# Mixer: a new order within a step for exponentials, products, taps and the shared kernels

## The reference

```
proj = rmsnorm(x) @ in_proj_w.T            # gate | hid, B, C | dt
hid, B, C = silu(causal_conv(hid_B_C))     # 4 taps along the tokens
L = exp(segsum(A * dt))                    # decay between tokens, per head
M = (C @ B.T) * L                          # per head; C @ B.T is shared by a group
y = M @ (hid * dt) + D * hid
yg = y * silu(gate); yg = yg * rsqrt(mean over a group of yg**2)
out = x + (yg * gnorm_w) @ out_proj_w.T
```

## Time and profile before

| | us |
|---|---|
| median of 3 runs | 2763.43 (2762.61 to 2765.62) |
| the profiled execution's own time | 2761.49 |
| its span in the trace | 2759.7 |
| TensorE busy | 2324.9 (84% of the span) |
| VectorE busy | 1963.2 (71%) |
| ScalarE busy | 1463.1 (53%) |
| GpSimd busy | 1210.6 (44%) |

### The profile page before, as it was taken

One profiled execution on the slowest core, in us unless ns is written; L12 is line 12 of the kernel. 1 busy time (PEld: TensorE's weight loads), 2 busy tenths in 40 slices (PEclk: granted clock), 3 DMA queues, 4 the chain that ended last, 5 costly groups with the idle time before them and its releaser, 6 DMA issues. The chain is left out here.

```text
span 2759.7 us, 33994 instructions
## 1 busy us (share of the span) xinstructions
PE 2324.9 (84%) x11172; PEld 1681.7 (61%) x11172; DVE 1963.2 (71%) x3158; ACT 1463.1 (53%) x3097; POOL 1210.6 (44%) x772
## 2 busy tenths in 40 slices
PE   5957767666523999999999999999999999889997
PEld 4532222225512767777767767777777777568996
DVE  4569989984434786686685685766765866778777
ACT  2344444433102795595685775866855956742221
POOL 2129988971000363363462553543634633541112
PEclk9989999988666999999999999999999999889999
DMA  2030030000041241231231321312312312220110
GB/s 80 22 123 0 0 122 0 0 28 34 27 152 64 90 124 54 73 118 49 86 95 54 96 83 61 110 55 79 111 55 72 115 54 73 73 78 24 47 47 31
DMA packets 117378, 183.59 MB, mean 67 GB/s; under 512 B 9760, under 2 KB 77728, under 8 KB 116192
## 3 DMA queue, kind: packets, MB, share of 16 engines
q1 hardware_dynamic: 117216, 181.55, 20.7%
HBM read 170.90 MB, written 10.62 MB: 66 GB/s over the span
## 5 line engine op out<-in xcount | busy, mean ns | idle before, releaser
L78 PE MATMUL mg_pb<-xT2h,mg_wh 128*128 128x512 f32 x1152 | 482.1, 419 | 17.0 <-POOL mg_wl L1265 17.0
L79 PE MATMUL mg_pb<-xT2l,mg_wh 128*128 128x512 f32 x1152 | 457.7, 397 | 0.0
L80 PE MATMUL mg_pb<-xT2h,mg_wl 128*128 128x512 f32 x1152 | 455.9, 396 | 0.0
L1275 POOL TENSOR_TENSOR mg_y<-mg_hT,mg_sg 128x512 f32<-128x512 f32 x128 | 175.6, 1372 | 633.7 <-DVE mg_hT L1510 633.7
L784 PE MATMUL ss_y<-ss_pr,cst 128*128 128x512 f32 x512 | 280.4, 683 | 123.5 <-POOL ss_pr L766 123.4
L1460 DVE SCALAR_TENSOR_TENSOR mg_hT<-mg_pb,mg_cw,mg_hT 128x510 f32<-128x510 f32 (+2 forms) x432 | 314.0, 739 | 30.3 <-ACT mg_hT L1615 24.6
L766 POOL TENSOR_TENSOR ss_pr<-o,ss_bc 128x1024 f32<-128x1024 f32 x128 | 301.3, 2369 | 46.2 <-DVE o L735 23.7
L1487 DVE TENSOR_TENSOR mg_m<-mg_gb,mg_cb 128x384 f32<-128x384 f32 x512 | 265.0, 549 | 74.8 <-ACT mg_gb L1665 72.2
L784 PEld LDWEIGHTS ss_y<-ss_pr,cst 128*128 128x128 f32 x512 | 100.0, 212 | 303.9 <-POOL ss_pr L766 222.0
L666 ACT ACTIVATE ss_da<-dt,ss_na 128x510 f32 (+1 forms) x256 | 165.9, 680 | 207.9 <-DVE o L735 207.9
L78 PEld LDWEIGHTS mg_pb<-xT2h,mg_wh 128*128 128x128 f32 x1152 | 220.1, 191 | 78.7 <-issue 18.8
(11 more groups left out here) (291 smaller groups left out, 5214.9 us busy)
## 6 DMA issues: line engine op xcount, KB each, us to landing
mg_abc<-acs_rows SPq DMA_DIRECT2D x256, 256.0 KB, 3.3
mg_ws<-in_w_in SPq DMA_DIRECT2D x72, 512.0 KB, 3.7
ss_bc<-bc_rows SPq DMA_DIRECT2D x16, 1024.0 KB, 6.3
mg_wos<-in_w_out SPq DMA_DIRECT2D x64, 256.0 KB, 4.0
ff_ws<-in_w SPq DMA_DIRECT2D x7, 1024.0 KB, 4.8
x<-in_x SPq DMA_DIRECT2D x16, 256.0 KB, 4.4
ip_ws<-in_w_in SPq DMA_DIRECT2D x8, 512.0 KB, 3.6
x_kept<-x SPq DMA_DIRECT2D x2, 2048.0 KB, 7.2
```

Of the source, the lines that this page charges most:

```text
L78: pe.matmul(out, lhs[0], rhs[0], start=start, stop=False)
L79: pe.matmul(out, lhs[0], rhs[1], start=False, stop=False)
L80: return pe.matmul(out, lhs[1], rhs[0], start=False, stop=stop)
L1275: pool.tensor_tensor(yb[:, p % RING, t], hT[s % 2][:, t], sg[s % 2][:, t], ALU.mult).then_inc(s_y2, 1)
```

## The change

The same operations are computed; only their places in the hand-written orders change, and one wait is added.

- VectorE, steps that finish a pair: `clamp(p, 1)` goes to the head of the step; products 2 and 3 come straight behind 0 and 1, ahead of the second `times_step` and of all taps; products 6 and 7 come ahead of the output tile's add and both skips; the second weight's low part goes behind the first skip. The taps of a half tile stay together.
- ScalarE there: decay 2 and 3 ahead of `high` and of the first tap; decay 6 and 7 ahead of the second `high`.
- B/C: the taps of C's second half (j = 3) and the four silus of B and C move into the next step, r = 1.
- r = 1 on TensorE: the first output tile ahead of `square_sums`, and `shared_kernels` behind the third projection. On VectorE `shared_out` goes behind the second `low`; on ScalarE `root` behind the second `high`.
- `clamp` waits for the group's table (`s_step`) where it is the first to need it.

```diff
--- before.py
+++ after.py
@@ -1429,13 +1429,12 @@
                     proj(s, 1, 0)
                     proj(s, 1, 1)
                     if outs:
+                        out_tile(*outs[0])
                         square_sums(s // PS - 1)
+                    proj(s, 2, 0)
+                    proj(s, 2, 1)
                     if not is_bc(s):
                         shared_kernels(s // PS)
-                    if outs:
-                        out_tile(*outs[0])
-                    proj(s, 2, 0)
-                    proj(s, 2, 1)
                     proj(s, 3, 0)
                     if outs:
                         out_tile(*outs[1])
@@ -1493,6 +1492,8 @@
                     g, q = divmod(p, PAIRS)
                     n = BATCH * p + b
                     dve.wait_ge(s_row[n % 3], 16 * (n // 3 + 1))
+                    if q == 0:
+                        dve.wait_ge(s_step, 16 * (g + 1))
                     for hh in range(2):
                         u = 2 * b + hh
                         if p * U + u >= 4:
@@ -1548,56 +1549,52 @@
                     p, outs, ow = turned_pair(s), out_tiles(s), new_out_weights(s)
                     bc = is_bc(s)
                     if p is not None:
+                        clamp(p, 1)
                         times_step(p, 0)
                         kernel_of(p, 0)
                         kernel_of(p, 1)
                         if ow:
                             low_weight(ow[0])
+                        kernel_of(p, 2)
+                        kernel_of(p, 3)
                         times_step(p, 1)
                         if outs:
                             low(*outs[0])
-                        clamp(p, 1)
-                        tap(1, s, 0)
-                        kernel_of(p, 2)
-                        kernel_of(p, 3)
-                        tap(2, s, 0)
-                        tap(3, s, 0)
-                        tap(1, s, 1)
+                        taps(s, 0)
                         kernel_of(p, 4)
                         kernel_of(p, 5)
                         clamp(p, 3)
-                        tap(2, s, 1)
-                        tap(3, s, 1)
-                        if ow:
-                            low_weight(ow[1])
+                        taps(s, 1)
+                        kernel_of(p, 6)
+                        kernel_of(p, 7)
                         if outs:
                             add(*outs[0])
                             low(*outs[1])
                         skip(p, 0)
+                        if ow:
+                            low_weight(ow[1])
                         if bc:
                             taps(s, 2)
-                        kernel_of(p, 6)
-                        kernel_of(p, 7)
                         if outs:
                             add(*outs[1])
                         skip(p, 1)
-                        if bc:
-                            taps(s, 3)
                         continue
                     if bc:
-                        for j in range(4):
+                        for j in range(3):
                             taps(s, j)
                         continue
                     if outs:
                         low(*outs[0])
+                    taps(s - 1, 3)
                     taps(s, 0)
                     if outs:
                         scales(outs[0][0])
                     taps(s, 1)
-                    shared_out(s // PS)
                     if outs:
                         add(*outs[0])
                         low(*outs[1])
+                    shared_out(s // PS)
+                    if outs:
                         add(*outs[1])
                 scales(NG - 1)
                 dve.wait_ge(s_rs, NG)
@@ -1691,28 +1688,25 @@
                     if p is not None:
                         decay(p, 0)
                         decay(p, 1)
+                        if ow:
+                            high_weight(ow[0])
+                        decay(p, 2)
+                        decay(p, 3)
                         if outs:
                             high(*outs[0])
-                        if ow:
-                            high_weight(ow[0])
                         first_tap(s, 0)
-                        decay(p, 2)
-                        decay(p, 3)
-                        first_tap(s, 1)
                         decay(p, 4)
                         decay(p, 5)
+                        first_tap(s, 1)
                         if ow:
                             high_weight(ow[1])
+                        decay(p, 6)
+                        decay(p, 7)
+                        if outs:
+                            high(*outs[1])
                         if bc:
                             first_tap(s, 2)
-                        if outs:
-                            high(*outs[1])
-                        decay(p, 6)
-                        decay(p, 7)
-                        if bc and s < NSTEP:
                             first_tap(s, 3)
-                            for j in range(4):
-                                silu(s, j)
                             continue
                         silu(s, 0)
                         silu(s, 1)
@@ -1722,17 +1716,18 @@
                     if bc:
                         for j in range(4):
                             first_tap(s, j)
-                        for j in range(4):
-                            silu(s, j)
                         continue
                     if outs:
                         high(*outs[0])
+                    silu(s - 1, 0)
+                    silu(s - 1, 1)
+                    silu(s - 1, 2)
                     first_tap(s, 0)
-                    if outs:
-                        root(outs[0][0])
+                    silu(s - 1, 3)
                     first_tap(s, 1)
                     if outs:
                         high(*outs[1])
+                        root(outs[0][0])
                     silu(s, 0)
                     silu(s, 1)
                     gate(s, 0)
```

## The result

| | before | changed |
|---|---|---|
| median, us | 2764.52 (2762.61 to 2765.98, 4 runs) | 2740.25 (2737.24 to 2741.54, 4 runs) |
| ratio to before | | 0.9915 [0.9901, 0.9929] |
| profiled execution, its span | 2761.49, 2759.7 | 2737.24, 2735.3 |

The kernel became faster by 24.3 us, where 15.4 were forecast. A later run of the same changed kernel, its last row in the table of experiments, gave 0.991 again. Which of the sum's terms were right is seen step by step.

The account below looks back on a forecast made before the run. TensorE, busy 84% of the span and nearly full in the mixer, was taken as the bound. Terms -45 - 3 + 24 + 8.4 = -15.4 us against 2761.49 gave 2746, as median 2748; range 2718 to 2772.

Parts of the forecast that it names:

- The B/C step: B/C steps: the 3.79 us wait for products and 2.6 us of clock loss go, seven times; -45 us.
- The weight steps: r = 5 to 8: the r = 6 wait mostly goes, others stay, since ScalarE has as much work as TensorE; -3 us.
- Clamp 1 at the head: Head clamps held by GpSimd delay times_step and TensorE's second turn, 1.1 us in each of 22 steps; +24 us.
- Low parts behind two more exponentials: r = 2: decay 2 and 3 delay high and low, so TensorE waits 1.2 us in seven steps; +8.4 us.
- Edits at nothing: Reordering inside r = 1, moving B and C silus there, and the added table wait were put at no cost.
- rival 2: Head clamps and weight-step clamp 3 each meet a whole GpSimd operation: +29 us, 2792, mostly near 2775; chance 0.17.
- rival 3: TensorE's clock also falls behind the new waits, 18 us in r = 2: 2766; chance 0.13 with a half-kept B/C wait.
- Rival 1: Clamps slip in front of GpSimd and all weight-step waits go: -54 us, 2709, or 2725 if about half; chance 0.2.

Follow-up runs that it names:

- B/C products late: Changed kernel with products 6 and 7 of the B/C step back behind the first skip and C's first three taps: 2766.5 us, ratio 1.0019.
- weight steps late: Changed kernel with products 6 and 7 back behind the first skip and second weight in r = 5 to 8: 2773.08 us, ratio 1.0043.
- GpSimd waits: Changed kernel, GpSimd's second-half gate product made to wait for the next pair's times_step in r = 0, 3 and 4: 2727.09 us, ratio 0.9873.
- clamp at the head alone: Kernel before with only clamp 1 (and its table wait) moved to the head of the step: 2775.23 us, ratio 1.0043.
- `high` first: Changed kernel, output tile's high part back ahead of decay 2 and 3, second times_step and low ahead of products 2 and 3: 2733.47 us, ratio 0.9898.
- C whole: Changed kernel with C's last taps and the B and C silus back in the B/C step, TensorE's new r = 1 order kept: 2772.19 us, ratio 1.0037.
- C whole, old r = 1: Changed kernel with C's last taps and silus back in the B/C step and TensorE's r = 1 order as before: 2758.7 us, ratio 0.9984.
- clamp behind the products: Changed kernel with clamp 1 behind products 0 and 1 and times_step instead of at the head: 2751.74 us, ratio 0.9964.

## Why the prediction was right, and where its sizes were off

The direction, the waits that go or come, and their places were right. That the sum came within 9 us is in part luck: the weight steps gave 10 us more than forecast, while r = 2 to 4 had a cost of some 6 us that the forecast did not have. (The printed terms add up to -15.6, not -15.4; the clamps' 22 times 1.1 is 24.2. This changes nothing.) By its own steps:

- **The B/C step, -45.** The 3.79 us wait went and with it the fall of the clock. With the second turn's cost in it, the seven stretches gave 39.0 us instead of 37.3. The head clamp's part was put at 1.1 us and measured 0.52 (turn 3.78): GpSimd's operations lay otherwise there, and the four clamps took 0.67, 0.28, 1.06 and 0.27 us. Without that part the step gave 42.6 us, where 45 were forecast. The run with the B/C products late shows the cause: a return of 2.33 us of wait, and a fall of the clock in five groups of seven, cost 26 us.
- **The weight steps, -3.** This term was mis-sized: -13.3. (Its own words, the r = 6 wait mostly gone, already give up to 6 us in seven groups.) The sentence that failed is that the exponentials give ScalarE a lead "in r = 5 only", with the other waits as they are. The windows give ScalarE 15.71 us of work in step r = 8, which takes 16.34, and its only wait is now 0.57 for the clamp; the 0.45 for the gate product is gone, and the one for the clamp grew from 0.37. So it still bounds that step, with 0.3 us less. But no wait of TensorE is left in r = 6 (15.58 us instead of 16.65), and 0.38 of it in r = 7 (16.17); in r = 8 0.54 remained. Products 6 and 7 late took 11.5 of the 13.3 us away again (15.58, 16.44, 16.67, 16.67) with ScalarE's new order in place, so the gain needs the early products. What they give with ScalarE's old order was not run.
- **Clamp 1 at the head, +24.** The mechanism was right, and shown by the run in which GpSimd waits. The 0.96 us at the turn is what was laid out. r = 3 and 4 cost 1.31 us each instead of 1.1. Without the hold they take 27.05, so the clamps are 14.4 us of the 18.3 in these steps, and the clamp at the head alone costs 1.0 per step on the kernel before.
- **Low parts behind two more exponentials, +8.4.** 0.98 us of wait and 1.37 us of step length against 1.2: +9.6. `high` first took 1.06 per step of it away, 7.1 us.
- **Edits at nothing.** C's split and the order of r = 1 showed no wait, as forecast. But they are not free to choose apart: C whole cost 32 us more than the changed kernel. One cost the forecast did not have at all: with products 6 and 7 ahead of the add and the second `low`, the second output tile starts late, 0.3 us in each of the 21 steps r = 2 to 4 of groups 1 to 7. That is the 6.3 us that the clamps' hold and `high` leave over.
- **The first group** stood nowhere in the sum. Its r = 3 met the split, as rival 2 had it for all places: clamp four took 2.37 us, the turn waited 2.67, and the clock fell once, which is rival 3's mechanism. The first group as a whole took only 2.4 us more, since other steps there gained.

Rows of that place in the changed kernel, VectorE, GpSimd, TensorE, and the two windows behind it:

```profile
935.46 2.37 DVE L1504 TENSOR_SCALAR mg_nd<-mg_abc,mg_tabs 128x128 f32<-128x128 f32 x1
...
935.36 2.39 POOL L1265 TENSOR_TENSOR mg_wl<-mg_ws,mg_wh 128x1024 fp32r<-128x1024 f32 x1
...
938.58 0.30 PE L1344 MATMUL mg_tb<-cst,mg_hT 128*128 128x128 f32 x1 [2.67 <-DVE mg_hc L1477]
...
938.58:943.00 4.42, 4.42 (x15) 3.59 (x16) 3.97 (x8) 4.01 (x13) 1.43 (x2) 0.61 0.53 177
943.00:946.00 3.00, 3.00 (x18) 2.02 (x17) 2.22 (x7) 1.55 (x4) 0.00 (x0) 1.00 0.39 79
```

Rival 1 was half right: most of the weight-step waits went, but two of the four clamps were still held in r = 3 and 4. Rival 2's longer hold is what the clamp alone meets on the kernel before, 1.0043. That the changed kernel escaped it in the B/C step is luck: the forecast had not worked it out, but had taken the pattern of the earlier trace rows for all places. Which of two like waits makes the clock fall stays open.

## What to carry to other kernels

Before moving a short operation of VectorE with its inputs in SBUF, look up which GpSimd operation it will lie beside at its new place, and beside which one the others will lie once GpSimd itself has moved: here the same edit cost 0.36 or 2.9 us depending on that, and in one run 2.7 us appeared in a step that nobody had edited. Where such a meeting is unavoidable, a wait on the engine with slack can be cheaper than a better place on the busy one (23 us for one line). And choose places step by step: the step lengths told which steps could bear the clamp at the head, and choosing by them, with `high` first, gave 27 us, where the change itself had given 24.

## What was not expected of the hardware

**The clock does not follow the length of a wait.** The granted clock (1.00 is 2.4 GHz, 0.50 is 1.2 GHz) in the two-microsecond windows behind each wait of TensorE in groups 1 to 7, counted over the places where it repeats:

| kernel, wait of | length, us | fell to the 0.50 level |
|---|---|---|
| before, last B/C products | 3.75 to 3.79 | 7 of 7 |
| C whole, output tile | 2.4 to 3.4 | 5 of 7 |
| clamp at the head alone, second turn | 2.9 | 7 of 7 |
| weight steps late, second turn | 2.7 | 2 of 7 |
| B/C products late, last products | 2.3 | 5 of 7 |
| C whole, old r = 1, square sums | 1.35 | 5 of 7 |
| clamp at the head alone, last products | 1.5 | 0 of 7 |
| clamp behind the products, a tap and an output tile | 1.5 to 1.65 | 0 of 14 |

Two groups of one execution, C whole, the six microseconds behind the same wait (3.39 and 3.34 us):

```profile
1454.31:1460.31 6.00, 6.00 (x28) 4.91 (x28) 2.09 (x3) 0.04 (x1) 2.20 (x1) 1.00 0.27 87
1648.64:1654.64 6.00, 6.00 (x15) 4.80 (x16) 2.10 (x3) 0.00 (x0) 2.18 (x1) 0.54 0.27 87
```

With the same busy time TensorE got 28 matmuls done in one and 15 in the other. Even two executions of one kernel differ: in the first group of the changed kernel the second turn waits 2.35 us in the one and 2.32 in the other, and the clock stayed at 1.00 in the first (r = 4 took 18.11 us) and fell in the second (19.63). The stretches give the price of a fall: in B/C products late 45.4 us without and 46.9 with it (48.35 once), in C whole 46.4 without and 48.9 with it, so 1.5 to 3 us. The Trainium skill (TensorE: Matmul & The Clock Gate, Part 1) says that the chip judges activity in windows that run on without regard to the kernel. The table agrees with it: behind a pause of one length the clock falls in one place and not in another. It is not shown what decides it; the square sums of C whole, old r = 1 are followed by small matmuls, which may have a part. The spread of the kernel with the B/C products late between executions, 2761.93 to 2773.68 us over 11, may come from that too; it was not tested.

**The hold has a pattern.** Of four clamps in a row beside a GpSimd engine without gaps, those held last until the operation beside them ends (1.06 to 1.34 us beside a whole operation of 128x512, 2.36 to 2.40 beside the subtraction of 128x1024, less where the clamp starts in its middle, as the 0.67 us in the B/C step). A clamp behind a held one takes 0.27 us where it starts in the 0.1 us before GpSimd's next operation, as the third at 1489.88 does; with the next operation already begun it is held too, as at 1622.36 in weight steps late (1.09 us). Products, whose one input comes from PSUM, are never held: each of the 512 takes 0.54 to 0.56 us in both kernels.
